# Gated attention and routed experts on one core: the order of work ahead of and in the slot loop

## Chip, cores and metric

The kernel runs on one NeuronCore of a Trainium2 chip. The metric is the time of one execution on the device, in microseconds (us); less is better.

## What is computed

The reference, cut to what matters here (B = 2, S = 512, D = 1024, 8 experts):

```python
def xattn(x1, x2):                      # per batch
    q1, q2 = fake_quant(x1, ...), fake_quant(x2, ...)
    return q1 @ q2
def ffn(x, W_gate, b_gate, W_e, b_e):
    logits = x @ W_gate + b_gate
    _, top_idx = top_k(logits, 2)
    y_all = relu(einsum('bsd,edh->bseh', x, W_e) + b_e)
    return take_along_axis(y_all, top_idx[..., None], axis=2).mean(axis=2)
x = x + tanh(g_xattn[0]) * xattn(layernorm(x), ctx)
x = x + tanh(g_ffn[0]) * ffn(layernorm(x), W_gate, b_gate, W_e, b_e)
```

## The kernel before, in words

The 1024 tokens are NT = 8 tiles of 128 rows, tiles 0 to 3 of the first batch (TPB = 4), 4 to 7 of the second. Per tile i the first part quantises x and the context, multiplies (attend, fold), adds to x (x_new, VectorE), takes the statistics (stats, scales), writes the normalised row y (normalise, ScalarE), stores y in DRAM (store_y, SP), transposes it on TensorE (transpose_y) and multiplies it with the gate's weights (gate).

Routing is done for two groups of four tiles, g = 0 and 1: select(g) finds the two best experts of every token on VectorE, counts(g) on TensorE counts by matmuls with a triangle of ones which place a token has among those of its expert, positions(g) reads that, and slot_matrix(g) (R) and make_onehot(i) make the operands with which place_rows on TensorE writes the list of tokens of each expert. A slot is 128 tokens of one expert: here 20 slots, numbered 0 to 19; slots 0 to 2 are expert 0's, and slots 3, 4, 6, 9, 13 and 16 are each the first of a next expert for which the one after it has still to be prepared (expert 7's slots come last).

Slots 0 and 1 don't wait for the whole list. oh_first (first_onehot, L906), the one-hot of the place in expert 0's column alone, gives by place_first the tokens of slot 0 from the first batch; first_rows writes their row numbers (sidx) and GpSimd gathers the rows of y (L517). ScalarE turns them from DRAM's order of quarters (put_in_order, L703), TensorE transposes them (turn_first), ScalarE writes yE_hi (evacuate_hi) and VectorE yE_lo (evacuate_lo): an fp32 product is made of three, hi by hi, hi by lo, lo by hi. place_second, second_rows and the gather at L522 do the same for slot 1, from both batches. products(q, ...) are the matmuls of slots 0 and 1.

Weights of an expert come in four pieces (chunks c) of 1 MB through stage. ScalarE writes w_hi from stage (split_hi), VectorE w_lo = stage - w_hi (split_lo, L944). Each of the two halves of w_hi and w_lo holds one expert. The half of w_hi for expert 1 lies in the same memory as xt, which holds x_new until its stores (store_x_new on SP, after add_rowsum on ScalarE for tiles 4 to 7) have landed (s_oi). The next piece of stage is loaded when both splits of the old one are done (load_w1 for expert 1).

From slot 2 on a loop runs on each engine, one step per slot, queue by queue: GpSimd gathers the rows of slot + 3 in four quarters (gather, L507) into one of two buffers, when ScalarE has written their numbers (gidx, pick_rows) and then adds the result to the output by an indirect DMA (scatter, L529). VectorE's step: yT_lo of slot + 1 (evacuate_lo, L938), the transposition of the rows of slot + 2 (turn_rows, L1067), in the first slot of an expert the four split_lo of the next expert, the bias (add_bias, L1072) when TensorE is done with the slot, relu and weight (weigh, L1076). ScalarE's step: when TensorE is done with slot - 1, yT_hi of slot + 1 (L687), gidx, and the four split_hi. TensorE: 48 matmuls of 512 columns a slot (L1419), which wait for yT_lo of the slot and piece by piece for w_lo. SP loads the four pieces of the expert after next as the splits free stage.

The order of every engine is written out by hand. Around the change it is, on VectorE:

```python
            x_new(7)
            stats(1, 7, 6)
            first_onehot(0)
            slot_matrix(0)
            scales(1, 7, 1, 6)
            first_rows()
```

and in VectorE's loop step:

```python
                turn_rows(q, turn + 1)
                with dve.If(nxt > 0):
                    for c in range(NCH):
                        split_lo(c, ...)
```

## Time and profile before

| | |
|---|---|
| time, median of 3 runs | 351.77 us (349.79 to 356.72) |
| the profiled execution | 349.38 us |
| its span | 347.6 us |
| mean granted clock of TensorE | 0.942 |
| busy: TensorE, VectorE, ScalarE, GpSimd | 90%, 70%, 42%, 50% |
| DMA | 81.48 MB, 234 GB/s |

The span runs from the first to the last instruction of the core; what is left of the execution's own time (1.8 us) lies around it. Busy shares are means over stages with different limits: the stage ahead of 131 us is many short instructions that wait for each other across engines, the loop behind it is mostly TensorE. An idle time in a timeline stands in brackets with the engine, tile and line that ended it; "issue" is time in which nothing that the profile shows was waited for. A piece of TensorE's timeline that starts before the last ends is no error, since matmuls are pipelined.

### The profile page before, as it was taken

Reading aid. Unit: us, or ns where it says so; the run is one execution under the profiler, and the core shown is the slowest. Engines: PE = TensorE matmul, PEld = TensorE weight load, DVE = VectorE, ACT = ScalarE, POOL = GpSimd, SP = SyncE. Lnnn points to the kernel's source line nnn. Section 1 sums busy time; section 2 is a strip of 40 time slices with the busy share of each in tenths; the row PEclk is TensorE's granted clock in tenths of the full one; section 3 lists DMA queues with packets and bytes.
Section 4 is the critical chain, followed back from the end, with each engine's and each line's share of the span. In section 5 each row is a group of like instructions: output and inputs, shape, how many; then the busy total and the mean of one; then the engine's idle time right before and its main releaser. Section 6 shows DMA issues by size and latency. Waiting matters only on the chain.

```text
span 347.6 us, 6194 instructions
## 1 busy us (share of the span) xinstructions
PE 311.7 (90%) x1591; PEld 238.8 (69%) x1598; DVE 244.2 (70%) x343; ACT 145.2 (42%) x144; POOL 174.3 (50%) x167
## 2 busy tenths in 40 slices
PE   4698999999899958999999979998999999999940
PEld 1243446769877837888888768877888888888830
DVE  2779999979669389598974965595639754964520
ACT  3768989854711461276446013701127114601100
POOL 5647534201010488684665566707748455847440
PEclk9989999988569996999999999999999999999995
DMA  6999937793726769889998995897559965546333
GB/s 222 414 410 385 389 122 240 300 312 117 201 104 184 285 227 326 248 246 414 315 387 206 334 326 121 184 367 241 121 121 256 396 142 154 125 71 154 63 86 60
DMA packets 19917, 81.48 MB, mean 234 GB/s; under 512 B 4160, under 2 KB 4160, under 8 KB 15808
## 3 DMA queue, kind: packets, MB, share of 16 engines
q1 hardware_dynamic: 12560, 58.76, 45.7%
q0 software_dynamic: 7200, 22.55, 28.4%
q8 instruction: 7, 0.11, 0.1%
q14 instruction: 6, 0.05, 0.0%
q10 hardware_dynamic: 144, 0.01, 0.0%
HBM read 62.43 MB, written 18.87 MB: 234 GB/s over the span
## 4 chain that ended last, share of the span: by engine, by line
PE 45%; DVE 23%; DMA 13%; issue 7%; ACT 4%; POOL 3%; DVEq 1%; SPq 1%; POOLq 0%; ACTq 0%
PE ps L1419 32%; DVE w_lo L944 8%; DMA out_dram<-res,sidx 4%; PE ps L1154 3%; DMA out_dram<-xt 3%; PE ps_q L1208 3%; PE ps_y L1183 2%; DVE st L771 2%; DMA stage<-in_ctx_dram 2%; DMA stage<-in_L_ffn_W_e_dram 2%; DVE res L1072 2%; PE ps_s L1208 2%; POOL y_rows L507 2%; DMA y_rows<-y_scratch,gidx 2%; DVE xt L827 1%
## 5 line engine op out<-in xcount | busy, mean ns | idle before, releaser
L507 POOL DMA_INDIRECT y_rows<-y_scratch,gidx x84 | 104.8, 1247 | 37.7 <-issue 25.3
L1419 PE MATMUL ps<-w_hi,yT_hi 128*128 x288 | 90.0, 394 | 8.7 <-DVE yT_lo L938 8.7
L1419 PE MATMUL ps<-w_lo,yT_hi 128*128 x288 | 89.6, 393 | 0.0
L1419 PE MATMUL ps<-w_hi,yT_lo 128*128 x288 | 89.4, 392 | 0.0
L687 ACT ACTIVATE yT_hi<-ps_y 128x1024 fp32r<-128x1024 f32 x20 | 20.5, 1027 | 132.8 <-PE ps L1419 76.8
L944 DVE TENSOR_TENSOR w_lo<-stage,w_hi 128x2048 f32 (+1 forms) x32 | 71.4, 2275 | 4.8 <-ACT w_hi L696 4.7
L1419 PEld LDWEIGHTS ps<-w_hi,yT_hi 128*128 128x128 f32 x288 | 54.4, 190 | 21.1 <-issue 10.1
L1419 PEld LDWEIGHTS ps<-w_hi,yT_lo 128*128 128x128 f32 x288 | 54.6, 190 | 11.5
L1419 PEld LDWEIGHTS ps<-w_lo,yT_hi 128*128 128x128 f32 x288 | 54.6, 190 | 11.5
L529 POOL DMA_INDIRECT out_dram<-res,sidx x20 | 32.3, 1616 | 59.3 <-DVE res L1076 47.5
L696 ACT ACTIVATE w_hi<-stage 128x2048 f32 (+1 forms) x28 | 51.6, 1906 | 5.9 <-DMA stage<-in_L_ffn_W_e_dram 3.5
L1072 DVE TENSOR_TENSOR res<-ps,bias 128x1024 f32<-128x1024 f32 x20 | 24.4, 1218 | 28.9 <-PE ps L1419 28.7
L1067 DVE STREAM_TRANSPOSE ps_y<-y_rows 128x1024 f32<-128x1024 f32 x20 | 25.2, 1260 | 21.7 <-DMA y_rows<-y_scratch,gidx 19.4
L1154 PE MATMUL ps<-q,q1T 128*128 128x512 bf16 x123 | 31.5, 394 | 1.0 <-DVE xt L827 0.5
L938 DVE TENSOR_TENSOR yT_lo<-ps_y,yT_hi 128x1024 fp32r<-128x1024 f32 x20 | 24.5, 1225 | 11.0 <-issue 8.2
L1154 PEld LDWEIGHTS ps<-q,q1T 128*128 128x128 bf16 x128 | 12.3, 101 | 16.0 <-issue 2.6
L771 DVE BATCH_NORM_STATS2 st<-xt 128x6 f32<-128x512 f32 x32 | 20.5, 682 | 0.4
L439 POOL TENSOR_SCALAR q<-u8c 128x1024 bf16<-128x1024 uint8 x14 | 14.9, 1069 | 9.2 <-ACT u8c L566 8.2
L566 ACT ACTIVATE u8c<-stage,par,drv 128x1024 uint8<-128x1024 f32 x14 | 16.7, 1229 | 0.8 <-DMA stage<-in_ctx_dram 0.8
L1076 DVE TENSOR_SCALAR res<-res,weight 128x1024 f32<-128x1024 f32 x18 | 13.7, 759 | 2.4
L1131 PE MATMUL ps<-fill,ident_b 128*128 128x512 bf16 x23 | 8.2, 522 | 4.8 <-POOL pick L433 4.8
L590 ACT ACTIVATE y<-xt,lnv 128x1024 f32<-128x1024 f32 x8 | 9.8, 1234 | 4.2 <-DVE lnv L796 4.2
(195 smaller groups left out, 295.3 us busy)
## 6 DMA issues: line engine op xcount, KB each, us to landing
stage<-in_L_ffn_W_e_dram SPq DMA_DIRECT2D x32, 1024.0 KB, 6.9
stage<-in_ctx_dram SPq DMA_DIRECT2D x16, 512.0 KB, 11.3
xt<-in_x_dram SPq DMA_DIRECT2D x8, 512.0 KB, 11.1
y_scratch<-y SPq DMA_DIRECT2D x8, 512.0 KB, 6.4
out_dram<-xt SPq DMA_DIRECT2D x8, 512.0 KB, 7.0
bias<-in_L_ffn_b_e_dram SPq DMA_DIRECT2D x8, 512.0 KB, 6.9
y_rows<-y_scratch,gidx POOLq DMA_INDIRECT x84
out_dram<-res,sidx POOLq DMA_INDIRECT x20
```

Of the source, the lines that this page charges most:

```text
L507: pool.indirect_dma_start(out=y_rows[q][:, b * QD:(b + 1) * QD], out_offset=None, in_=y_quarters[:, :], in_offset=bass.IndirectOffsetOnAxi ...
L529: pool.indirect_dma_start(out=out_rows[:, :], out_offset=bass.IndirectOffsetOnAxis(ap=sidx[:, q:q + 1], axis=0), in_=res[q][:, :], in_offs ...
L687: act.activation(into[:, :, :], ps_y[:, :, :], ACT.Copy).then_inc(s_eh, 1)
L696: act.activation(w_hi[:, bass.ds(half * WSZ + c * CW, CW)], stage[:, CK * c:CK * (c + 1), :].rearrange("p k h -> p (k h)"), ACT.Copy).then ...
L771: last = dve.bn_stats(st[:, which, h, :], xt[:, i, h * 512:(h + 1) * 512])
L938: dve.tensor_tensor(into[:, :, :], ps_y[:, :, :], hi[:, :, :].bitcast(f32), ALU.subtract).then_inc(s_el, 1)
L944: dve.tensor_tensor(w_lo[:, dst], stage[:, CK * c:CK * (c + 1), :].rearrange("p k h -> p (k h)"), w_hi[:, dst].bitcast(f32), ALU.subtract) ...
L1067: dve.transpose(ps_y[:, :, :].rearrange("p k (b r) -> p k b r", b=NQ), y_rows[q][:, :].rearrange("p (b k r) -> p k b r", b=NQ, k=KT)).then ...
L1072: dve.tensor_tensor(res[q][:, :], ps[q][:, :], bias[:, bass.ds(half * D, D)], ALU.add).then_inc(s_free, 1)
L1154: pe.matmul(ps[slab(i)][:, h * 512:(h + 1) * 512], q1T[:, i, k % KT, :], q2[:, k, h * 512:(h + 1) * 512], start=(k % KT == 0), stop=False)
L1208: last = pe.matmul(into, yT[YT_HOME[i]][:, k, :], wg[:, k, :], start=(k == 0), stop=(k == KT - 1))
L1419: last = pe.matmul(ps[q][:, h * 512:(h + 1) * 512], lhs[q][:, k, :], w[:, bass.ds(woff + k * D + h * 512, 512)], start=(k == 0 and lhs is ...
```

## The change

Edits of order and one of layout:

- VectorE, ahead of the loop: first_onehot(0) and slot_matrix(0) come ahead of x_new(7); first_rows is cut in two (row numbers early, weights later); split_lo(3) of expert 0 moves from behind evacuate_lo(0) to ahead of select(1).
- oh_first has the tile as its innermost index in place of the outermost, so place_first and place_second read their stationary operand with a step of 4 elements.
- TensorE: counts(0) ahead of the last four attends of tile 7; place_first directly behind fold(7); turn_first(0) ahead of gate(7), with its wait for keep_yT(7); place_rows of tile 3 and place_second one product later or earlier.
- ScalarE: the ordered rows of slot 0 and yE_hi ahead of the four add_rowsum; split_hi(0) of expert 1 ahead of evacuate_hi(1).
- SP: y of tiles 6 and 7 ahead of the third load of expert 1, and the stores of x_new ahead of its fourth.
- VectorE, in the loop: two of the four split_lo ahead of turn_rows and two behind it, each pair under its own test of nxt.

```diff
-        oh_first = [at(f"oh_first{b}", [P, TPB, P], bf16, WLO + 38 * KB + KB * b) for b in range(B)]
+        oh_first = [at(f"oh_first{b}", [P, P, TPB], bf16, WLO + 38 * KB + KB * b) for b in range(B)]
...
             for e in range(2):
                 load_bias(e)
-            store_y(5)
+            for i in range(TPB + 1, NT):
+                store_y(i)
             load_w1(2)
-            store_y(6)
-            store_y(7)
-            load_w1(3)
             for i in range(TPB, NT):
                 store_x_new(i)
+            load_w1(3)
...
-            for i in range(TPB, NT - 1):
-                add_rowsum(i)
             act.wait_ge(s_first, 16)
             put_in_order(0, res[0])
-            add_rowsum(NT - 1)
             evacuate_hi(0, yE_hi)
+            for i in range(TPB, NT):
+                add_rowsum(i)
             act.wait_ge(s_g[1], 16)
             put_in_order(1, y_rows[1])
+            act.wait_ge(s_oi, 16 * NT)
+            split_hi(0, 1, 32)
             evacuate_hi(1, yT_hi[1])
...
-            act.wait_ge(s_oi, 16 * NT)
-            for c in range(NCH):
+            for c in range(1, NCH):
                 split_hi(c, 1, 32)
...
-                dve.tensor_tensor(oh_first[b][:, :, :], pL[:, r, 0:1].to_broadcast([P, TPB, P]),
-                                  iota_pe[:, :, 0].unsqueeze(1).to_broadcast([P, TPB, P]), ALU.is_equal).then_inc(s_ohf, 1)
+                dve.tensor_tensor(oh_first[b][:, :, :], pL[:, r, 0].unsqueeze(1).to_broadcast([P, P, TPB]),
+                                  iota_pe[:, :, 0:TPB], ALU.is_equal).then_inc(s_ohf, 1)
...
                 rows_of(0, fl(V1F), A0)
+
+            def first_weights():
+
                 dve.tensor_scalar(fl(W0), fl(V1F), 0.0, dv(C2), ALU.is_lt, ALU.mult)
...
             dve.wait_ge(s_iota, 1)
-            x_new(7)
-            stats(1, 7, 6)
             first_onehot(0)
             slot_matrix(0)
+            x_new(7)
+            first_rows()
+            stats(1, 7, 6)
+            make_onehot(0)
             scales(1, 7, 1, 6)
-            first_rows()
-            for i in range(TPB):
+            first_weights()
+            for i in range(1, TPB):
                 make_onehot(i)
             split_lo(2, 3, slice(2 * CW, 3 * CW))
             read_rowsums(1)
+            split_lo(3, 4, slice(3 * CW, 4 * CW))
             select(1)
...
             evacuate_lo(0, yE_lo)
-            split_lo(3, 4, slice(3 * CW, 4 * CW))
...
                 dve.wait_ge(s_el, slot + 2)
+                def split_some(first, end):
+                    with dve.If(nxt > 0):
+                        for c in range(first, end):
+                            split_lo(c, nxt * NCH + c + 1, bass.ds((nxt & 1) * WSZ + c * CW, CW))
+
+                split_some(0, NCH // 2)
                 turn_rows(q, turn + 1)
-                with dve.If(nxt > 0):
-                    for c in range(NCH):
-                        split_lo(c, nxt * NCH + c + 1, bass.ds((nxt & 1) * WSZ + c * CW, CW))
+                split_some(NCH // 2, NCH)
...
             transpose_y(4)
+            counts(0)
             attend_quarters(7, 2, 4)
-            counts(0)
             fold(7)
+            place_first()
             transpose_y(5)
             gate(4)
             transpose_y(6)
             gate(5)
-            place_first()
             gate(6)
...
             place_rows(0, 0, 1)
+            pe.wait_ge(s_ye, NT)
+            turn_first(0)
             gate(7)
             place_rows(0, 1, 3)
-            pe.wait_ge(s_ye, NT)
             counts(1)
-            turn_first(0)
-            place_rows(0, 3, TPB)
...
-            products(0, yE_hi, w_hi, 0, 3)
+            products(0, yE_hi, w_hi, 0, 2)
+            place_rows(0, 3, TPB)
             place_second()
-            products(0, yE_hi, w_hi, 3, KT)
+            products(0, yE_hi, w_hi, 2, KT)
```

TensorE's queue from gate(7) on, before (yT_66 is the transposed y of tile 7, onehot_90 to 92 those of tiles 1 to 3, in_order_74 the ordered rows of slot 0):

```order
L1208 MATMUL ps_q<-wg,yT_66 128x8 x8
L1275 MATMUL ps<-R,onehot_90 128x8 x8
L1275 MATMUL ps<-R,onehot_91 128x8 x8
L1221 MATMUL ps_s<-sel,before 128x40
L1224 MATMUL ps_s<-sel,ones_b 128x40 x4
L1224 MATMUL ps_s<-sel,ones_b 128x32
L1224 MATMUL ps_s<-sel,ones_b 128x24
L1224 MATMUL ps_s<-sel,ones_b 128x16
L1224 MATMUL ps_s<-sel,ones_b 128x8
L1256 MATMUL ps_y<-ident_f,in_order_74 128x128 x8
L1275 MATMUL ps<-R,onehot_92 128x8 x8
L1263 MATMUL ps<-w_hi,yE_hi 128x512 x6
```

And after:

```order
L1264 MATMUL ps_y<-ident_f,in_order_74 128x128 x8
L1216 MATMUL ps_q<-wg,yT_66 128x8 x8
L1283 MATMUL ps<-R,onehot_90 128x8 x8
L1283 MATMUL ps<-R,onehot_91 128x8 x8
L1229 MATMUL ps_s<-sel,before 128x40
L1232 MATMUL ps_s<-sel,ones_b 128x40 x4
L1232 MATMUL ps_s<-sel,ones_b 128x32
L1232 MATMUL ps_s<-sel,ones_b 128x24
L1232 MATMUL ps_s<-sel,ones_b 128x16
L1232 MATMUL ps_s<-sel,ones_b 128x8
L1271 MATMUL ps<-w_hi,yE_hi 128x512 x4
L1283 MATMUL ps<-R,onehot_92 128x8 x8
```

The transposition of slot 0's rows is now ahead of gate(7) and of the counts that follow from it, and the last one-hot has gone behind the first four matmuls of slot 0.

VectorE's queue in a step of the loop, behind yT_lo, before (y_rows_56 are the gathered rows, ps_y their transposition; the ISA and REGISTER rows are its sequencer's):

```order
L938 TENSOR_TENSOR yT_lo_55<-ps_y,yT_hi_53 128x1024
L1065 ISA
L1067 STREAM_TRANSPOSE ps_y<-y_rows_56 128x1024
L1106 REGISTER_ALU x2
L1106 COMPARE_AND_BRANCH
L943 ISA
L944 REGISTER_ALU
L944 ISA
L944 TENSOR_TENSOR w_lo<-stage,w_hi 128x2048
L943 REGISTER_ALU
L944 ISA
L944 TENSOR_TENSOR w_lo<-stage,w_hi 128x2048
```

And after:

```order
L1110 REGISTER_ALU x2
L1110 COMPARE_AND_BRANCH
L945 ISA
L946 REGISTER_ALU
L946 ISA
L946 TENSOR_TENSOR w_lo<-stage,w_hi 128x2048
L945 REGISTER_ALU
L946 ISA
L946 TENSOR_TENSOR w_lo<-stage,w_hi 128x2048
L1110 UNCONDITIONAL_BRANCH
L1069 ISA
L1071 STREAM_TRANSPOSE ps_y<-y_rows_56 128x1024
```

The first pair of splits, with the branch and its registers, stands ahead of the transposition, and a second branch opens behind it.

ScalarE's queue behind the last keep_yT, before:

```order
L608 ACTIVATE xt<-xt,rsum 128x1024 x3
L703 ACTIVATE in_order_74<-res_58 128x512 x2
L608 ACTIVATE xt<-xt,rsum 128x1024
L687 ACTIVATE yE_hi<-ps_y 128x1024
L703 ACTIVATE res_58<-y_rows_57 128x512 x2
L687 ACTIVATE yT_hi_53<-ps_y 128x1024
L717 TENSOR_LOAD tab
```

And after:

```order
L702 ACTIVATE in_order_74<-res_58 128x512 x2
L686 ACTIVATE yE_hi<-ps_y 128x1024
L607 ACTIVATE xt<-xt,rsum 128x1024 x4
L702 ACTIVATE res_58<-y_rows_57 128x512 x2
L695 ACTIVATE w_hi<-stage 128x2048
L686 ACTIVATE yT_hi_53<-ps_y 128x1024
L717 TENSOR_LOAD tab
```

The ordered rows and yE_hi are ahead of all four rows of x_new, and one piece of w_hi stands ahead of yT_hi of slot 1 (yT_hi_53).

## Rows read from the trace of the kernel before

**Rows 1.** The page, section 2: granted clock of TensorE in 40 slices of 8.7 us.

```profile
PEclk9989999988569996999999999999999999999995
```

**Rows 2.** The chain that ended last, its longest piece (start us, us, what).

```profile
235.63 98.23 PE ps L1419 x432
```

**Rows 3.** Timeline of TensorE, the loop: start us, us, instruction, [idle before <-releaser].

```profile
131.24 1.22 PE L1419 MATMUL ps<-w_hi,yT_hi 128*128 x2 [5.22 <-DVE yT_lo L938]
...
201.76 0.73 PE L1419 MATMUL ps<-w_hi,yT_hi 128*128 x2 [2.52 <-DVE yT_lo L938]
...
235.63 0.72 PE L1419 MATMUL ps<-w_hi,yT_hi 128*128 x2 [0.92 <-DVE yT_lo L938]
```

**Rows 4.** Timeline of VectorE ahead of slot 2.

```profile
120.81 2.29 DVE L944 TENSOR_TENSOR w_lo<-stage,w_hi 128x2048 fp32r<-128x2048 f32 x1 [4.73 <-ACT w_hi L696]
...
127.14 1.25 DVE L1067 STREAM_TRANSPOSE ps_y<-y_rows 128x1024 f32<-128x1024 f32 x1
```

**Rows 5.** Timeline of ScalarE ahead of slot 2.

```profile
116.38 0.32 ACT L691 ACTIVATE gidx<-qidx 128x4 uint32 x2 [1.66 <-issue]
118.86 7.33 ACT L696 ACTIVATE w_hi<-stage 128x2048 fp32r<-128x2048 f32 x4 [2.16 <-DMA out_dram<-xt]
```

**Rows 6.** Timeline of SP's queue.

```profile
108.02 2.35 SPq L340 DMA_DIRECT2D out_dram<-xt  x4
```

**Rows 7.** Windows: stretch, length, busy of PE, PEld, DVE, ACT, POOL (x), PEclk, DMA, GB/s.

```profile
131.20:136.40 5.20, 5.16 (x12) 4.13 (x13) 4.78 (x3) 1.12 (x2) 4.29 (x4) 0.51 1.05 294
137.00:142.20 5.20, 5.20 (x25) 4.26 (x24) 2.87 (x3) 0.00 (x0) 3.94 (x4) 1.00 1.08 362
...
201.80:207.00 5.20, 5.20 (x23) 4.31 (x24) 3.73 (x5) 1.23 (x2) 3.98 (x5) 1.00 1.04 321
```

**Rows 8.** Timeline of VectorE, the step of slot 6.

```profile
187.66 1.26 DVE L1067 STREAM_TRANSPOSE ps_y<-y_rows 128x1024 f32<-128x1024 f32 x1 [4.94 <-DMA y_rows<-y_scratch,gidx]
```

**Rows 9.** Timeline of ScalarE, weights of slots 4 and 6.

```profile
161.85 1.92 ACT L696 ACTIVATE w_hi<-stage 128x2048 f32 x1 [1.21 <-DMA stage<-in_L_ffn_W_e_dram]
...
179.63 7.32 ACT L696 ACTIVATE w_hi<-stage 128x2048 f32 x4
```

**Rows 10.** Timeline of VectorE, steps of slots 2 to 5.

```profile
143.03 1.26 DVE L1067 STREAM_TRANSPOSE ps_y<-y_rows 128x1024 f32<-128x1024 f32 x1 [1.86 <-DMA y_rows<-y_scratch,gidx]
...
147.31 1.23 DVE L938 TENSOR_TENSOR yT_lo<-ps_y,yT_hi 128x1024 fp32r<-128x1024 f32 x1 [0.23 <-issue]
...
164.25 8.86 DVE L944 TENSOR_TENSOR w_lo<-stage,w_hi 128x2048 f32 x4
...
175.42 1.22 DVE L938 TENSOR_TENSOR yT_lo<-ps_y,yT_hi 128x1024 fp32r<-128x1024 f32 x1 [0.23 <-issue]
```

**Rows 11.** Timeline of TensorE, start of slot 6.

```profile
177.27 0.63 PE L1419 MATMUL ps<-w_hi,yT_hi 128*128 x2
```

**Rows 12.** Timeline of GpSimd's queue, first gather of slot 4.

```profile
131.54 2.24 POOL L507 DMA_INDIRECT y_rows<-y_scratch,gidx  x1 [0.30 <-issue]
```

**Rows 13.** Timeline of TensorE ahead of slot 0's products.

```profile
88.72 3.57 PE L1208 MATMUL ps_q<-wg,yT 128*128 128x8 f32 x16
...
94.86 0.19 PE L1221 MATMUL ps_s<-sel,before 128*128 128x40 bf16 x1 [1.61 <-issue]
...
95.13 1.95 PE L1256 MATMUL ps_y<-ident_f,in_order 128*128 128x128 f32 x8
96.87 0.64 PE L1275 MATMUL ps<-R,onehot 128*128 128x8 f16 x8
98.28 2.90 PE L1263 MATMUL ps<-w_hi,yE_hi 128*128 128x512 f32 x6 [0.78 <-ACT yE_hi L687]
```

**Rows 14.** Groups by line and form, 76 to 112 us: oh_first.

```profile
L906 DVE TENSOR_TENSOR oh_first<-pL,iota_pe 128x512 bf16<-128x512 bf16 x2 | 2.2, 1084 | 0.1
```

**Rows 15.** DMA issues, us to landing: slot 0's gather.

```profile
res<-y_scratch,sidx POOLq DMA_INDIRECT x1, 5.1
```

**Rows 16.** Timeline of VectorE: slot 0's row numbers.

```profile
84.64 0.15 DVE L915 TENSOR_SCALAR sidx<-early 128x1 uint32<-128x1 f32 x1
```

More of the change, by code:

```diff
@@ L1237, in place_first @@
                     for c in (0, TPB):
-                        last = pe.matmul(first_in, oh_first[0][:, i, :], R[:, i * E, c:c + 1],
+                        last = pe.matmul(first_in, oh_first[0][:, :, i], R[:, i * E, c:c + 1],
                                          start=(i == 0 and c == 0), stop=(i == TPB - 1 and c == TPB))
@@ L1246, in place_second @@
                 for i in range(NT):
-                    last = pe.matmul(second_in, oh_first[i // TPB][:, i % TPB, :], R[:, i * E, 0:2],
+                    last = pe.matmul(second_in, oh_first[i // TPB][:, :, i % TPB], R[:, i * E, 0:2],
                                      start=(i == 0), stop=(i == NT - 1))
```

## The prediction

> **What bounds the kernel now.** I read the page first, then the timeline of TensorE for its gaps, then the timelines of the engines that ended them, and last the windows for the granted clock. The page shows the clock at full speed but for the stretch ahead of slot 0's products and a dent near 130 us [rows 1]. From slot 11 on TensorE never waits: one piece of 432 matmuls from 235.63 to 333.98 us [rows 2]. A slot is 48 matmuls, so 98.23 / 9 = 10.9 us. Nothing in the last nine slots can be won by order; what can be won lies ahead of them, in three gaps inside the slot loop [rows 3] and on the way to the first of them.
>
> Gap A, 5.22 us ahead of slot 2. It ends with yT_lo of slot 2 on VectorE, which follows the transposition of y_rows at 127.14, which stands behind the first two w_lo pieces of expert 1; the first of these waited 4.73 us for w_hi [rows 4]. ScalarE could write that w_hi only at 118.86, when the stores of x_new had landed (2.16 us of wait are put to out_dram) [rows 5]: expert 1's w_hi lies where x_new lay. The stores went out at 108.02 [rows 6], because SP stood at the fourth load of expert 1 ahead of them, which waits for VectorE's last split of expert 0. Gap A also costs clock: in the 5.2 us behind it 12 matmuls run at 0.51 of full speed, against 25 in as long a stretch later. That is 2.4 us lost [rows 7].
>
> Gap B, 2.52 us ahead of slot 8, ends with yT_lo of slot 8. In VectorE's step for slot 6, the first of an expert, the transposition waited 4.94 us for gathered rows until 187.66 [rows 8], and the four w_lo pieces stood behind it. Gap C, 0.92 us ahead of slot 11, has the same form. After gap B the clock stayed full [rows 7].
>
> **The change part by part.**
>
> *Two w_lo pieces ahead of the transposition in the loop.* Four pieces take 8.86 us [rows 10], so two take 4.4. From 182.7 VectorE runs them in place of waiting: ScalarE writes w_hi from 179.63 at 1.83 us a piece [rows 9], two by 183.3, so they hardly wait. They end at 187.2, the rows are there at 187.66, the other two end near 193.3 instead of 197.7. yT_lo of slot 8 is written by about 197, before the end of slot 7 at 199.1. Gap B goes: -2.52. Gap C too: the gather behind it is issued after the scatter of an earlier slot, which now goes out some 4 us sooner: -0.92. The slow first pairs after both gaps (0.73 and 0.72 against 0.63 [rows 3, 11]) give 0.2. What is late next is TensorE itself. In steps whose rows are there at once the transposition comes 4.4 us later; its reader, ScalarE's yT_hi, waits for the end of TensorE's slot anyway, and of the 10.9 us about 1.2 us of cover stay. Bounds: -3.6 to 0.
>
> *The price in the loop.* Each step tests its branch twice. Before, the branch is issued while the transposition runs; now the first stands open behind the wait for yT_lo. No row shows it; the nearest is the 0.23 us of issue ahead of yT_lo [rows 10]. I take 0.3 us a step, between 0 and three times that row.
>
> *Where that price decides.* Slots 3 and 4 are each the first of an expert. VectorE works through both steps without a pause: from yT_lo at 147.31 to the end of yT_lo for slot 6 (175.42 + 1.22) are 29.3 us [rows 10], and with the 0.53 us of hand-over that lies between yT_lo's end and the first matmul after gap A it allows slot 6 at 177.17; TensorE began it at 177.27 by its own work [rows 11]. Slack 0.1 us. This stretch is VectorE's own work, which the change reorders but doesn't shorten. So any head start that TensorE wins before slot 6 is lost there, unless the stretch itself begins sooner. It begins when the rows of slot 4 are there: the transposition at 143.03 waited 1.86 us for them [rows 10]. They come from GpSimd's queue, which from 116.85 on issues twelve gathers and a scatter nearly end to end, the last four from 131.54 [rows 12]. The queue starts when ScalarE writes gidx at 116.38 [rows 5], behind the second turn_first.
>
> *Ahead of the loop: does gidx come sooner?* counts(0) ahead of the last attends gives VectorE its input 1.6 us sooner. first_onehot and the slot matrix, now ahead of x_new 7, end near 78.7 and put it off by 0.2. The new layout of oh_first is read and written in steps that no row shows; between the old 1.08 us [rows 14] and half of it, I take 0.9, near the one row there is. TensorE has place_first behind fold(7), waits there some 0.4 us and begins transpose_y(5) about 0.8 us late; so comes all behind it, turn_first(0) at 89.7. Slot 0's gather follows sidx, now at 80.6 instead of 84.64 [rows 16]; at 5.1 us from issue to landing [rows 15] the rows lie there by 87, and ScalarE orders them straight behind the last keep_yT, from 89.4 to 90.5. turn_first(0), 1.95 us at half clock, ends at 91.8; gate(7), 3.57 us, which stood ahead of it and ended at 92.28, now ends at 95.2. From gate(7) to counts(1) are 2.6 us of select on VectorE (92.28 to 94.86), so counts(1) comes at 97.8 and slot 0's products at 98.2, against 98.28 [rows 13]. What the early yE_hi wins, the late select gives back: 0. place_rows of tile 3, 0.64 us [rows 13], now stands behind the start of the products; with the 0.1 won it shifts slots 0 and 1, turn_first(1) and gidx by 0.4 to 0.5 (gidx 116.8). Bounds: -1.3 to +1.3, by whether 1.95 + 0.64 us of this run at half or at full clock.
>
> The Trainium skill, SBUF — State Buffer, "Door 1: The DMA port swizzle", says that accesses which each cross into a new 16-byte line pay a penalty. By it the new oh_first, which still reads pL in such steps, would stay at 1.08 us and place_first be 0.2 later. No row here shows the new layout.
>
> *Stores and loads in their new order, split_lo(3) early.* split_lo(3), 2.3 us, falls into VectorE's wait for gate(7): free. The stores of x_new go out from 94 to 97.5 and land by 105. ScalarE writes the first w_hi of expert 1 near 109.5, behind the ordered rows of slot 1 (it is ahead of yT_hi(1) in its queue, which needs turn_first(1) at 113.1, so it holds nobody). VectorE's first split then runs at 116.9 instead of 120.81 and the second at 121.2. The transposition of slot 2 now waits for its gather: four issues of 1.25 us from 117.2, two of them a us longer since they lie beside splits (as the 2.24 us in [rows 12]), landing near 125.8. With the 4.1 us from transposition to matmul [rows 3, 4], slot 2 begins at 129.9: a wait of 3.4 us instead of 5.22. If the clock holds, slot 3 begins 3.4 us sooner than before and slot 6 could at 174. But GpSimd's queue starts 0.4 us later and has as many splits beside it, four, so the rows of slot 4 are there at 143 as before, and slot 6 begins at 177.17 + 0.6 (two branches): +0.5 against 177.27. The head start is worth nothing.
>
> *Clock.* TensorE waits 3.4 us ahead of slot 2 and 3 us or so ahead of slot 6. It fell after a wait of 5.22 us and not after 2.52 [rows 3, 7]. A fall ahead of slot 2 costs nothing (slot 6 covers it); one at slot 6 costs the 2.4 us above. I give it one in four: +0.6.
>
> The Trainium skill, TensorE: Matmul & The Clock Gate, "HAM oscillation — how this bites in real kernels", says that waits between bursts of matmuls throttle the array again, so that each burst starts cold. By it slot 6 would start cold and the sum be 1.8 us more. The trace has one wait that did this and one that didn't.
>
> **Sum**, against the profiled execution (349.38 us, of it 347.6 span): -2.52 - 0.92 - 0.2 + 0.5 + 0.6 = -2.5, so 346.8. The median of the runs shown is 351.77, the lowest 349.79, 0.4 over the profiled one; I add 1.0 for that spread: 347.8.
>
> **The rivals.**
> 1. *The head start survives*, because GpSimd's queue or the splits go faster than I sum. For it: in what started the stretch, the rows of slot 4 were only some 0.3 us ahead of TensorE. Against it: twelve gathers end to end. 347.8 - 3.4 - 0.6 = 343.8.
> 2. *The gaps return as one.* Those of slots 8 and 11 go, but the wait ahead of slot 6 has the branches at their upper bound (1.4 for 0.5) and the clock falls there in full (2.4 for 0.6): 347.8 + 0.9 + 1.8 = 350.5.
> 3. *Slower: the transposition behind two splits holds TensorE.* It must end before TensorE's slot does and now ends 9.7 us into 10.9. In slot 4 ScalarE waited for the weights themselves, 1.21 us for the second piece [rows 9]. Where w_hi of the first two pieces comes over 1.2 us later than VectorE asks for it, each further us is one of TensorE. With 3 us beyond that in four of the six steps: 347.8 + 12 = 360. Against it: at 179.63 all four w_hi go end to end (7.32 us) [rows 9].
> 4. *It doesn't do what it says:* sidx of slot 0 is early, but turn_first(0) waits on PE for the ordered rows, holds gate(7), and select(1), gidx and slot 6 come 3 us later: 347.8 + 3 = 350.8.
>
> **How the numbers follow.** Forecast 0.52, rival 1 0.19, rival 2 0.14, rival 3 0.05, rival 4 0.10. Range 343.0 to 352.0: it takes in rivals 1, 2 and 4 with the spread of the runs. Some 2% (7 us) is what a measurement of this kernel can tell from no change. Faster by more asks for 344.7 or less, rival 1 and little else: 0.20. Slower by more: rival 3 and a tail of 4, 0.06. Within it: 0.74.
>
> **What would show it.** Right: no wait of TensorE ahead of slots 8 and 11 and a transposition without wait in slot 6; stores of x_new out before 100; slot 0's products within 1 us of 98.3; slot 2 near 130; a new wait of 2 to 4 us ahead of slot 6, which starts between 177 and 178.5. Wrong: slot 6 before 176 without a wait (rival 1), ScalarE's yT_hi waiting for the transposition in expert steps with TensorE idle (rival 3), gidx after 118 (rival 4).

## The result and the profile after

| | before | after |
|---|---|---|
| median (range) of 9 runs each, us | 351.17 (349.79 to 356.72) | 353.82 (350.61 to 355.25) |
| ratio, 95% interval | | 1.0082 (1.0048 to 1.0115) |
| profiled execution, its span, us | 349.38, 347.6 | 353.82, 352.0 |
| mean granted clock | 0.942 | 0.932 |

The change makes the kernel slower by 0.8%, where 347.8 us was forecast. The interval lies above 1, but the loss is less than the 2% that the prediction names as what a measurement can tell. Medians are over all runs of a kernel, while ratios and intervals, on both sides, leave out the runs that are more than 1.5% above the fastest of their kernel. Each ratio is against the kernel before on the same chip, whose own median lies between 351.2 and 353.4 us.

The two profiles overstate the difference. That of after is its median run, that of before lies 1.8 us below its median; of the 4.4 us between them, 2.65 lie between the medians.

The page's clock row answers to [rows 1]: the dip is wider, and the one near 140 us is still there.

```profile
PEclk9999999986557997899999999999999999999995
```

TensorE's timeline of the loop answers to [rows 3] (start us, us, instruction, [idle before <-releaser]); no other row of the loop has a wait.

```profile
138.22 1.21 PE L1427 MATMUL ps<-w_hi,yT_hi 128*128 x2 [6.56 <-DVE yT_lo L940]
...
185.26 0.72 PE L1427 MATMUL ps<-w_hi,yT_hi 128*128 x2 [0.80 <-DVE yT_lo L940]
```

The waits ahead of slots 8 and 11 are gone, and from slot 6 to the end of the span now lie 352.0 - 185.26 = 166.7 us against 347.6 - 177.27 = 170.3 [rows 11]: -3.6. But slot 2 starts at 138.22 instead of 131.24 and slot 6 at 185.26 instead of 177.27. The loss lies ahead of slot 2. TensorE's timeline there answers to [rows 13]:

```profile
78.80 0.40 PE L1246 MATMUL ps<-R,oh_first 128*128 128x1 f16 x8 [0.65 <-issue]
...
81.68 1.62 PE L1191 MATMUL ps_y<-ident_f,y 128*128 128x128 f32 x8
83.09 6.83 PE L1216 MATMUL ps_q<-wg,yT 128*128 128x8 f32 x32
...
93.47 1.94 PE L1264 MATMUL ps_y<-ident_f,in_order 128*128 128x128 f32 x8 [0.38 <-ACT in_order L702]
95.21 3.42 PE L1216 MATMUL ps_q<-wg,yT 128*128 128x8 f32 x16
98.47 1.09 PE L1283 MATMUL ps<-R,onehot 128*128 128x8 f16 x16
101.16 0.21 PE L1229 MATMUL ps_s<-sel,before 128*128 128x40 bf16 x1 [1.59 <-DVE sel L855]
...
101.45 2.05 PE L1271 MATMUL ps<-w_hi,yE_hi 128*128 128x512 f32 x4
103.31 0.67 PE L1283 MATMUL ps<-R,onehot 128*128 128x8 f16 x8
104.33 0.40 PE L1255 MATMUL ps_s<-R,oh_first 128*128 128x2 f16 x8 [0.36 <-DVE R L891]
104.59 5.20 PE L1271 MATMUL ps<-w_hi,yE_hi 128*128 128x512 f32 x12
```

The waits ahead of the first product are near those foreseen (0.65 ahead of place_first, 0.38 for the ordered rows, 1.59 for select); the 0.36 us that place_second (L1255) waits for R was not foreseen. Nor were the durations: gates 5 and 6 (83.09) take 6.83 us together, where one gate at half clock was 3.57 us before [rows 13], and the twelve products at 104.59 still run at half clock. Windows of 1 us give the two edges (columns as in [rows 7]); of after

```profile
82.00:83.00 1.00, 1.00 (x7) 1.00 (x6) 0.93 (x4) 0.24 (x1) 0.61 (x1) 0.52 0.08 33
109.00:110.00 1.00, 1.00 (x5) 0.84 (x4) 0.86 (x6) 0.00 (x0) 0.00 (x0) 0.83 0.65 213
```

and of before

```profile
85.00:86.00 1.00, 1.00 (x8) 1.00 (x8) 0.97 (x3) 0.41 (x1) 0.31 (x1) 0.54 0.02 8
102.00:103.00 1.00, 1.00 (x6) 0.83 (x5) 0.96 (x5) 0.00 (x0) 0.00 (x0) 0.92 0.00 0
```

A mean of 0.54 in a window that ends at 0.50 means a fall 0.08 us into it; a mean of 0.92 that began at 0.50 a return 0.16 us into it. So the clock was at its lower level (1.2 of 2.4 GHz) from 85.1 to 102.2 before, and from 82.0 to 109.3 after: 27.3 us for 17.1. In both kernels TensorE was busy all through the window in which it fell.

The lower clock isn't one profile's accident. The mean granted clock of every run is on record: 0.922 to 0.941 in the nine runs of after (mean 0.930), and 0.923 to 0.952 in the 65 runs of the kernel before that were made beside the experiments (mean 0.936, and 0.935 to 0.937 on each of their chips). Span times mean clock, an estimate of the span at full clock throughout, is 326.8 us in the mean for after and 328.1 for before. By this estimate the changed kernel has 1.3 us less to do, and the lower clock costs it some 2.4 us.

In the two profiles slot 1 ends 5.6 us late (131.65 for 126.03). The other 1.4 us up to slot 2 are its longer wait, 6.56 us for 5.22. GpSimd's queue, the first gathers of the loop:

```profile
121.24 0.95 POOL L506 DMA_INDIRECT y_rows<-y_scratch,gidx  x1 [13.43 <-ACT gidx L690]
122.50 2.23 POOL L506 DMA_INDIRECT y_rows<-y_scratch,gidx  x1 [0.30 <-issue]
125.03 0.95 POOL L506 DMA_INDIRECT y_rows<-y_scratch,gidx  x1 [0.30 <-issue]
126.28 2.57 POOL L506 DMA_INDIRECT y_rows<-y_scratch,gidx  x1 [0.30 <-issue]
```

SP's queue (after [rows 6]), and VectorE's transposition (after [rows 4]):

```profile
97.53 3.45 SPq L340 DMA_DIRECT2D out_dram<-xt  x4
...
124.08 19.68 SPq L382 DMA_DIRECT2D stage<-in_L_ffn_W_e_dram  x4
```

```profile
134.10 1.26 DVE L1071 STREAM_TRANSPOSE ps_y<-y_rows 128x1024 f32<-128x1024 f32 x1 [6.07 <-DMA y_rows<-y_scratch,gidx]
```

The stores leave 10.5 us sooner, as intended, and the transposition no longer stands behind splits. But the last of the four gathers is issued at 126.3 to 128.85, behind the first load of expert 2 (124.08), and its rows are there only at 134.1, 5.2 us after the issue ended.

Between slots 2 and 6 another 1.0 us goes. VectorE's timeline of slots 4 to 8:

```profile
154.71 1.23 DVE L940 TENSOR_TENSOR yT_lo<-ps_y,yT_hi 128x1024 fp32r<-128x1024 f32 x1 [0.24 <-issue]
156.53 4.50 DVE L946 TENSOR_TENSOR w_lo<-stage,w_hi 128x2048 f32 x2 [0.60 <-DVE yT_lo L940]
...
183.49 1.23 DVE L940 TENSOR_TENSOR yT_lo<-ps_y,yT_hi 128x1024 fp32r<-128x1024 f32 x1 [0.23 <-issue]
...
197.70 1.25 DVE L1071 STREAM_TRANSPOSE ps_y<-y_rows 128x1024 f32<-128x1024 f32 x1
```

In the same step of the kernel before, yT_lo was followed by the transposition:

```profile
148.79 1.26 DVE L1067 STREAM_TRANSPOSE ps_y<-y_rows 128x1024 f32<-128x1024 f32 x1 [0.26 <-DVE yT_lo L938]
```

The chain from yT_lo of slot 4 to the end of that of slot 6 takes 183.49 + 1.23 - 154.71 = 30.0 us, against 29.3: the branch shows as 0.60 us behind yT_lo instead of 0.26, once for slot 4 and once for slot 5. The transposition at 197.70 (slot 6's step) has no wait, where before it had 4.94 [rows 8].

The account of the two profiles: +5.6 (slot 1 ends) +1.4 (longer wait) +1.0 (to slot 6) -3.6 (slots 8 and 11) = +4.4 us of span, 352.0 - 347.6.

### The profile page after: what moved, and what is told of

Read it like the earlier page. It is cut to its first block, busy times and chain, and to the rows that moved or that the text cites. A ratio compares the mean times of both kernels' runs of the same rounds, so it can differ in the third digit from the quotient of the medians.

```text
span 352.0 us, 6225 instructions
## 1 busy us (share of the span) xinstructions
PE 316.5 (90%) x1597; PEld 242.6 (69%) x1598; DVE 243.9 (69%) x343; ACT 144.8 (41%) x144; POOL 189.8 (54%) x167
## 3 DMA queue, kind: packets, MB, share of 16 engines
q0 software_dynamic: 7200, 22.55, 27.9%
## 4 chain that ended last, share of the span: by engine, by line
PE 64%; DVE 15%; DMA 6%; ACT 4%; issue 4%; POOL 2%; DVEq 1%; ACTq 1%; SPq 0%; POOLq 0%
PE ps L1427 47%; PE ps L1271 3%; PE ps_q L1216 3%; PE ps L1162 3%; PE ps_y L1191 3%; DMA stage<-in_L_ffn_W_e_dram 2%; DMA y_rows<-y_scratch,gidx 2%; DVE st L770 2%; DMA stage<-in_ctx_dram 2%; PE ps_s L1216 2%; DVE w_lo L946 2%; DVE xt L826 1%; ACT u8c L565 1%; POOL y_rows L506 1%; ACT w_hi L695 1%
## 5 line engine op out<-in xcount | busy, mean ns | idle before, releaser
L506 POOL DMA_INDIRECT y_rows<-y_scratch,gidx x84 | 118.4, 1410 | 39.4 <-issue 25.0
L1427 PE MATMUL ps<-w_lo,yT_hi 128*128 x288 | 89.6, 392 | 0.0
L528 POOL DMA_INDIRECT out_dram<-res,sidx x20 | 34.3, 1714 | 43.0 <-DVE res L1080 30.9
L1080 DVE TENSOR_SCALAR res<-res,weight 128x1024 f32<-128x1024 f32 x18 | 13.9, 771 | 2.4
L521 POOL DMA_INDIRECT y_rows<-y_scratch,sidx x1 | 1.4, 1400 | 23.8 <-DVE sidx L914 23.8
L596 ACT ACTIVATE yT<-ps_y 128x1024 f32<-128x1024 f32 x8 | 8.2, 1020 | 12.7 <-PE ps_y L1191 12.6
```

The lines of the kernel that those rows point to most:

```text
L506: pool.indirect_dma_start(out=y_rows[q][:, b * QD:(b + 1) * QD], out_offset=None, in_=y_quarters[:, :], in_offset=bass.IndirectOffsetOnAxi ...
L528: pool.indirect_dma_start(out=out_rows[:, :], out_offset=bass.IndirectOffsetOnAxis(ap=sidx[:, q:q + 1], axis=0), in_=res[q][:, :], in_offs ...
L1427: last = pe.matmul(ps[q][:, h * 512:(h + 1) * 512], lhs[q][:, k, :], w[:, bass.ds(woff + k * D + h * 512, 512)], start=(k == 0 and lhs is ...
```

## The experiments

**The loop edit alone, and all without it.** The first is the kernel before with this, the second the changed kernel without it:

```diff
-                turn_rows(q, turn + 1)
-                with dve.If(nxt > 0):
-                    for c in range(NCH): split_lo(c, ...)
+                split_some(0, NCH // 2)
+                turn_rows(q, turn + 1)
+                split_some(NCH // 2, NCH)
```

> Only the loop edit: two w_lo pieces ahead of the transposition, two behind, all else as before. Theory A (the loss lies ahead of the loop, the loop edit pays as its terms say): the waits ahead of slots 8 and 11 (2.52 and 0.92 us) go, slot 6 begins 0.5 to 0.8 us later with a wait of that size, so 2.5 to 3 us less than before, ratio 0.992. Theory B (the loop edit itself costs: the second branch and w_hi waits in six steps): at least 2 us more than before, ratio 1.006 or above.

> Everything of the change but the loop edit. Theory A: slot 2 begins 6 to 7 us later than before and the waits ahead of slots 8 and 11 are back, 0 to 3.5 us of them; time 5 to 8 us over before, ratio 1.015 to 1.022. Theory B: all of the change's loss is the loop's, ratio 1.00.

Measured: 348.09 us, ratio 0.987 (0.978 to 0.997), and 357.21 us, ratio 1.010 (1.000 to 1.020). Alone, slot 6 starts 1.0 us later (178.24) and no wait of TensorE over 0.4 us is left behind it; without it the wait ahead of slot 8 is back (2.58 us). The edit pays, as theory A says. The rest of the change loses, but less than theory A's 1.015 to 1.022, and the interval touches 1; slot 2 did start 7.8 us late in its profile (139.05).

**The order of TensorE and VectorE ahead of slot 0 (the front, from here on) as before.** SP's and ScalarE's order, the early split_lo(3) and the loop edit stay. The edit, cut (make_onehot(0), counts(0) and place_first go back too):

```diff
-            first_onehot(0); slot_matrix(0); x_new(7); first_rows(); ...
+            x_new(7); stats(1, 7, 6); first_onehot(0); slot_matrix(0); ...
-            turn_first(0)
             gate(7)
             place_rows(0, 1, 3)
             counts(1)
+            turn_first(0)
+            place_rows(0, 3, TPB)
-            products(0, yE_hi, w_hi, 0, 2)
-            place_rows(0, 3, TPB)
+            products(0, yE_hi, w_hi, 0, 3)
```

> The change with the order of TensorE and VectorE ahead of slot 0's products put back (x_new 7, stats, first_onehot, place_first, gate(7), counts(1), turn_first(0), place_rows as before); the early split_lo(3), SP's and ScalarE's order and the loop edit stay. Theory A1 (the clock's earlier fall comes from the new front): half clock begins near 85 again, slot 0's products near 98.3, slot 1 ends near 126; the time falls to 345 to 348. Theory A2 (the clock's fall wanders from run to run by itself, whatever the order): products as late as 101 in some, time as after within 2 us. Theory C (slot 2's rows land late because the gather lies beside expert 2's load): a wait of 4 to 6 us ahead of slot 2 in spite of w_hi being ready, and slot 2 not before 130.

Measured: 349.5 us (345.5 to 352.7), ratio 0.989 (0.983 to 0.995), against 1.008: these two orders carry the loss. With the loop edit alone the ratio was 0.987, so the early stores, ScalarE's order and the early split_lo(3) show no gain. The time lies between the forecasts of A1 and A2, and the one profile looks like A2: its clock fell at 82.6 and its products began at 100.41. Theory C came true: slot 2 still waited 6.29 us.

**Expert 2's load behind slot 2's gather**, in the changed kernel and in the last one.

```diff
             sp.wait_ge(s_tab, 1)
+            sp.wait_ge(s_g[0], 16 * NQ)
             with sp.Fori(2, E) as n:
```

> The change, and SP's first load of expert 2 waits until slot 2's rows have landed. Theory C: the transposition for slot 2 begins 3 to 5 us after the gather's first issue plus 4 issues, near 130.5 instead of 134.1, TensorE's wait ahead of slot 2 is 2.5 to 3.5 us instead of 6.56 and slot 2 begins at about 134.5; slot 6 gains less, 1 to 3 us. Rival (the rows are late because GpSimd's own issue is slow beside the splits): transposition at 133 or later in spite of the free queues, and time as after or above.

> e3_front_undone, and SP's first load of expert 2 waits until slot 2's rows have landed. Theory C (the gather for slot 2 loses to the 1 MB load): wait ahead of slot 2 about 3 us instead of 6.29, clock not or hardly lowered there, time 1.5 to 3 us under e3 for the same fall of the clock ahead of slot 0. Theory of the prediction (a head start is lost in VectorE's steps for slots 3 and 4): of the 3 us at slot 2 at most 2 are left at the start of slot 6, which has a wait ahead of it.

Measured: 353.03 us, ratio 1.007 (1.000 to 1.014), and 349.95, ratio 0.995 (0.986 to 1.004). VectorE's and TensorE's timelines of the first:

```profile
130.66 1.26 DVE L1072 STREAM_TRANSPOSE ps_y<-y_rows 128x1024 f32<-128x1024 f32 x1 [2.62 <-DMA y_rows<-y_scratch,gidx]
```

```profile
134.81 0.72 PE L1428 MATMUL ps<-w_hi,yT_hi 128*128 x2 [3.17 <-DVE yT_lo L941]
...
148.26 0.72 PE L1428 MATMUL ps<-w_hi,yT_hi 128*128 x2 [2.26 <-DVE yT_lo L941]
...
183.10 0.73 PE L1428 MATMUL ps<-w_hi,yT_hi 128*128 x2 [1.88 <-DVE yT_lo L941]
```

With gather issues at the same times (the last ends at 128.86) the transposition finds its rows 1.8 us after the issue instead of 5.2, and the wait ahead of slot 2 is 3.17, near the 3.4 forecast. With the old order ahead of slot 0 it falls from 6.29 to 3.30. So it is the load that the gather loses to. But slots 3 and 6 now wait. Of the 3.4 us won at slot 2 in the first profile, 2.2 are left at slot 6 (183.10 for 185.26) and 1.1 at the end of the span; the clock fell once more behind slot 6 (184.3 to 187.7). In the second, counted from the end of slot 1, it is 3.0, 1.8 and 1.4. So in the profiles the head start is about halved, not lost, and the forecast that it is worth nothing isn't borne out as it stands. The median of the second (349.95) is no lower than without the wait (349.5), where 1.5 to 3 us were expected.

**Slot 0's products in one piece**: in the changed kernel with the load behind the gather; in the changed kernel by itself; and, the other way round, the broken order (4 matmuls, place_rows, place_second, the rest) put into the kernel before with the loop edit.

```diff
             place_rows(0, 1, 3)
+            place_rows(0, 3, TPB)
             counts(1)
-            products(0, yE_hi, w_hi, 0, 2)
-            place_rows(0, 3, TPB)
+            products(0, yE_hi, w_hi, 0, 3)
             place_second()
-            products(0, yE_hi, w_hi, 2, KT)
+            products(0, yE_hi, w_hi, 3, KT)
```

> e4_load_behind_gather, and place_rows of tile 3 stands ahead of counts(1) (in the wait for select) and place_second behind three steps of products, so that slot 0's products begin with 6 matmuls and one short break. Theory D (the clock comes back late because slot 0's products are broken up after 4 matmuls): half clock ends 4 to 6 us behind the first product instead of 7.6, slot 1 ends 1.5 to 2.5 us sooner than in e4 (131.6), time 1 to 2 us under e4. Rival (the clock's return follows only where its own steps happen to fall): first product to return anything from 4 to 8 us, time within 1 us of e4.

> The changed kernel, of it only slot 0's products as before: place_rows of tile 3 ahead of counts(1), three products (6 matmuls) in front of place_second. The load of expert 2 is where the change has it. Theory (the four matmuls in front of the small place_rows and place_second keep the clock low for longer): the clock is back at full by 103 to 105 instead of 109.2, slot 1 ends near 127 instead of 131.65, the time is 347.5 to 350.5, ratio to the kernel before 0.985 to 0.995. Rival (where the clock falls wanders from run to run, 82 to 86 us, and the order of the products has no part in it): back within 8 us of the first product whether it fell early or late, time 352 to 355, ratio 1.0 to 1.01.

> The kernel before with the loop edit, and slot 0's products in the changed order: two products (4 matmuls), place_rows of tile 3, place_second, then the rest. Nothing else of the front is touched. Theory (the broken products hold the clock down): the clock is back 7 us or more behind the first product (106 or later, before 102.1 with the first product at 98.3), slot 1 ends 2 to 4 us later than in the kernel with the loop edit alone, time 350 to 352, ratio 0.993 to 1.0. Rival (the wandering of the fall alone): back near 102, time 348, ratio 0.983 to 0.99.

Measured: 347.58 us, ratio 0.988 (0.980 to 0.997), where the same kernel with broken products had 1.007 (1.000 to 1.014); 350.93, ratio 1.000 (0.997 to 1.003), where the changed kernel had 1.008 (1.005 to 1.012); and 350.39, ratio 0.992 (0.988 to 0.995), where the loop edit alone had 0.987 (0.978 to 0.997). With the new order ahead of slot 0 whole products are faster, clear of the noise; with the old one the intervals overlap, and nothing is shown.

The profiles say only in part why. TensorE's timeline with the load behind the gather and broken products:

```profile
81.66 1.75 PE L1192 MATMUL ps_y<-ident_f,y 128*128 128x128 f32 x8
83.19 6.84 PE L1217 MATMUL ps_q<-wg,yT 128*128 128x8 f32 x32
...
93.58 1.94 PE L1265 MATMUL ps_y<-ident_f,in_order 128*128 128x128 f32 x8 [0.39 <-ACT in_order L703]
```

and with whole ones:

```profile
81.66 1.07 PE L1192 MATMUL ps_y<-ident_f,y 128*128 128x128 f32 x8
82.57 3.95 PE L1217 MATMUL ps_q<-wg,yT 128*128 128x8 f32 x32
...
90.06 1.94 PE L1265 MATMUL ps_y<-ident_f,in_order 128*128 128x128 f32 x8 [0.40 <-ACT in_order L703]
...
98.05 2.91 PE L1272 MATMUL ps<-w_hi,yE_hi 128*128 128x512 f32 x6
```

Up to the transposition of the ordered rows both have the same instructions, and at 81.66 they are at the same place to 0.01 us. Yet the clock fell at 81.9 in one and at 85.7 in the other, and that alone makes 3.5 us (93.58 to 90.06). The order of the products comes behind the fall and can't have moved it in that execution. All profiles of kernels without idle matmuls, by windows of 1 us ("broken" or "whole" are slot 0's products; the front is the new one unless the name says undone, before or loop edit alone):

| kernel | fell | first product | back, after first product | slot 1 ends, after first product |
|---|---|---|---|---|
| before | 85.1 | 98.28 | 3.9 | 27.8 |
| loop edit alone | 85.3 | 98.18 | 4.2 | 27.9 |
| front undone | 82.6 | 100.41 | 6.1 | 28.8 |
| front undone, load behind gather | 84.8 | 98.63 | 3.3 | 27.8 |
| load behind gather, products whole | 85.7 | 98.05 | 4.8 | 28.3 |
| products whole, by itself | 87.3 | 99.50 | 4.9 | 28.3 |
| after (broken, as the next two) | 82.0 | 101.45 | 7.9 | 30.2 |
| all but the loop edit | 83.3 | 102.84 | 7.7 | 30.1 |
| load behind gather | 81.9 | 101.56 | 7.6 | 30.1 |
| loop edit alone, products broken | 83.2 | 97.05 | 6.6 | 29.3 |

(The front undone was profiled in a somewhat longer execution, 350.89 us.) With whole products the clock is back after 3.3 to 6.1 us, with broken ones after 6.6 to 7.9. From first product to the end of slot 1 that is 29.3 to 30.2 us for 27.8 to 28.8; 0.67 of it is place_rows, which only changed sides, so the broken order goes with some 1.1 us.

That it is the cause is not quite shown, since the two groups also differ in when the clock fell. All four profiles with broken products are among those with an early fall (81.9 to 83.3); the one with whole products and as early a fall (82.6) needed 6.1 us, not far from the 6.6. One pair is free of this: from the fall to the first product are 13.8 us in "front undone, load behind gather" and 13.9 in "loop edit alone, products broken", and the clock was back 3.3 us behind the first product with whole products and 6.6 with broken ones. It is one pair.

The third kernel was expected to have its clock back at 106 or later, which its early first product did not allow (103.7), and slot 1 to end 2 to 4 us later than with the loop edit alone; it ended 0.2 us later (126.3), in a profile in which all of this part stood 1.5 us earlier. The median meets the 350 to 352. Its profile shows a stall of 3.3 us that no other has (VectorE in slot 3, put to a remote event), so its span decides nothing. The second kernel had its clock back at 104.4, as its theory says, but 350.93 lies between the theory's range and the rival's. The first gained 5.5 us where 1 to 2 were expected, and 3.5 of them are, in the profiles, the later fall.

Does the fall have a place of its own in either order? By the clock of the profile it fell at 82.0, 83.3, 81.9, 85.7, 87.3 with the new front, and at 85.1, 85.3, 82.6, 84.8, 83.2 with the old. Three profiles stand 1.3 to 1.5 us later or earlier than their likes at place_first already (80.12, 80.29 and 81.79). With that taken off the falls are 81.9 to 82.0 in the three with the new front and broken products, 85.7 and 85.8 in the two with whole ones, and 82.6 to 85.3 in the five with the old front. That may be chance or something that goes with the kernel; with one profile a kernel it stays open. Between the runs of one kernel the clock differs as well: the nine means of after, 0.922 to 0.941, stand for 41 to 55 us at half clock (an estimate, twice the missing share times the span).

**Idle matmuls against the fall of the clock.** They write a bank that the next real matmul clears and add nothing to the result. Four kernels have them: the changed kernel with the load behind the gather; the kernel before with the loop edit; the changed kernel with the old front; and the changed kernel with whole products and the load behind the gather. The edit in the first, without the 3 ahead of place_first:

```diff
             gate(5)
+            keep_clock(4, ps[1][:, 0:512])
             gate(6)
+            keep_clock(4, ps[1][:, 0:512])
...
             place_rows(0, 0, 1)
+            keep_clock(4, ps[0][:, 0:512])
...
             gate(7)
+            keep_clock(4, ps[0][:, 0:512])
             place_rows(0, 1, 3)
+            keep_clock(4, ps[0][:, 0:512])
```

> e4_load_behind_gather with idle matmuls of 512 columns (ones times identity into a bank that is free there) put between the gates: 3 ahead of place_first, 4 each behind gate(5), gate(6), the first place_rows, gate(7) and the next place_rows; 23 in all, 5 us at full clock. Theory A (what is lost ahead of slot 0 is clock, because TensorE has only short matmuls there): no fall of the clock between 78 and 110 or a much shorter one; slot 0's products begin by 97 instead of 101.4, slot 1 ends by 123 to 126 instead of 131.6, time 5 or more us under e4. Rival (the stretch is bound by the waits between engines, and the clock only looks like the cause): products begin at 101 or later.

> The kernel before with the loop edit alone (e1_loop_alone), and the same idle matmuls: 4 each behind gate(5), gate(6), the first place_rows, gate(7) and the next place_rows, 3 ahead of slot 0's products. Theory A: the clock holds here too, slot 0's products begin by 95 instead of 98.2, slot 1 ends by 120 to 122, time 3 to 6 us under e1 and less spread between runs. Rival: they cost their 5 us and give nothing, time at or over e1.

> The changed kernel with the order of TensorE and VectorE ahead of slot 0 as before (early stores of x_new, early split_lo(3), ScalarE's order and the loop edit kept), and idle matmuls that hold the clock: 4 of 512 columns each behind gate(5), gate(6), the first place_rows, gate(7) and the next place_rows, 3 ahead of the products. Theory (the only thing wrong with the changed kernel is the clock ahead of slot 0, and the head start on slot 2 is capped by VectorE's chain of slots 3 and 4): 344.5 to 346.5, no better than the old front with the loop edit and the same idle matmuls (345.05). Rival (the early stores are worth something once the clock is held): 342 to 344.

> The changed kernel with SP's wait for the gather, slot 0's products unbroken, and idle matmuls of 512 columns that hold the clock (3 ahead of place_first, 4 each behind gate(5), gate(6), the first place_rows, gate(7), and ahead of counts(1)). Theory (the loss of the change is the clock ahead of slot 0; with it held, VectorE's chain through slots 3 and 4 is what is left, and it sets slot 6 at 176 to 178.5 whatever the head start): 344.5 to 347.5, ratio 0.978 to 0.987, as good as the old front with the loop edit and idle matmuls (345.05) and not better. Rival (with the clock held, the early yE_hi and early splits are worth their 3 us): 341 to 343.5, slot 6 before 175.

Measured, in this order: 348.22 us, ratio 0.987 (0.978 to 0.997), where the same kernel without them had 1.007 (1.000 to 1.014); 345.05, ratio 0.979 (0.970 to 0.988), the fastest of all, where the loop edit alone had 0.987 (0.978 to 0.997); 354.9, with five of six runs at 354.3 to 356.4 and one at 348.44, which is inconclusive; and 349.73, ratio 0.985 (0.979 to 0.990), with seven runs from 345.8 to 352.6 and one at 464.6 (mean clock 0.642), which no profile explains. TensorE's timeline of the second:

```profile
88.45 2.34 PE L1212 MATMUL ps_q<-wg,yT 128*128 128x8 f32 x16
...
98.11 1.62 PE L1267 MATMUL ps<-w_hi,yE_hi 128*128 128x512 f32 x6
...
99.79 2.52 PE L1267 MATMUL ps<-w_hi,yE_hi 128*128 128x512 f32 x10
```

and two of its windows:

```profile
89.00:90.00 1.00, 1.00 (x9) 1.00 (x9) 0.00 (x0) 1.00 (x1) 0.00 (x0) 0.82 0.70 106
96.00:97.00 1.00, 1.00 (x11) 1.00 (x10) 0.96 (x2) 0.06 (x1) 0.00 (x0) 0.77 0.65 266
```

The clock still fell, but for a shorter time: from 89.6 to 96.5 here, where it was down from 85.3 to 102.4 with the loop edit alone, and from 97.0 to 100.4 in the first kernel, where it was down from 81.9 to 109.2. The six first products take 1.62 us instead of 2.90 [rows 13]. They begin no sooner (98.11 for 98.18; by 95 was expected), since the idle matmuls take the time that the clock gives back, and slot 1 ends 1.7 us sooner (124.39; 120 to 122 was expected). In the first kernel products begin at 98.74 instead of 101.56 and slot 1 ends 4.9 us sooner (126.73). So the half clock ahead of slot 0 is real time in the new order, clear of the noise; in the old one the intervals overlap, though three of the four runs (344.8 to 345.1) lie under all four with the loop edit alone (347.2 to 350.1); the fourth took 352.4.

The new order ahead of slot 0 is not shown to be faster than the old one when both have idle matmuls: 0.985 against 0.979, with overlapping intervals. Nor is this a comparison at full clock. The one profile of the fourth kernel, of a run of 351.34 us, has the clock down from 87.5 to 97.7 and from 101.1 to 104.5, its products begin at 103.64, and slot 6 starts at 183.00, outside the 176 to 178.5 of its theory. In the second kernel slot 6 starts at 176.34, 1.9 us sooner than with the loop edit alone. What holds in all of these is the length of VectorE's chain (30.0 us from yT_lo of slot 4 to the end of that of slot 6 in after, with the loop edit alone, with the load behind the gather, and in this second kernel); where it begins moves.

## Why the prediction was wrong

**The step that failed** is "Ahead of the loop", its sum "What the early yE_hi wins, the late select gives back: 0 ... Bounds: -1.3 to +1.3, by whether 1.95 + 0.64 us of this run at half or at full clock". It took the place where the clock falls (85 us) from one profile and let only two instructions move across it. After's fall at 82.0 put gates 5 and 6, the transposition and all up to the products at half clock: first product at 101.45, not 98.2, and gidx at 120.77, not 116.8. Over the runs the clock's share is smaller but there: mean 0.930 against 0.936, some 2.4 us by the estimate above. As an order of instructions the step was about right: where the clock fell at 85.7 the products of the new order began at 98.05.

**Second, in the same step**, place_rows of tile 3 behind the first products was costed at its own 0.64 us. With it the clock came back 7.9 us behind the first product instead of 3.9, and place_second waited 0.36 us for R: 30.2 us to the end of slot 1 instead of 27.8. Whole products brought the ratio from 1.008 to 1.000, and from 1.007 to 0.988 with the load behind the gather. How much of the late return is due to the broken order, and how much to the early fall, is not settled. A profile of before, in which the products are whole, has no row for that.

**Third, "landing near 125.8" and slot 2 at 129.9 with a wait of 3.4 us.** With the load out of the way the wait is 3.2 to 3.3 and slot 2 starts at 129.6 to 129.9 where the products start near 98. In the changed kernel expert 2's load leaves ahead of the last gather, and the wait is 6.56. I counted each queue's issues and took the landing from a stretch where no load ran beside it. The same paragraph has the rows of slot 4 "at 143 as before"; they were there at 149.27 in after, 4.4 us of it by the late gidx and 1.9 by a later landing behind gidx.

**The base.** The sum starts from a profiled execution of 349.38 us and adds 1.0 us for the spread of the runs. The median of nine is 351.17, so 1.8 was due; this term is 0.8 us of the 6.0 us by which the forecast missed.

**Right:** the waits of slots 8 and 11 (-3.6 forecast and measured); 0.3 us a branch (0.34); the stores (97.53); select's lateness (1.59 us ahead of counts(1)). oh_first takes 1.03 and 1.06 us in its new layout and took 1.08: my 0.9 was off by 0.15. By the Trainium skill, SBUF — State Buffer, "Door 1: The DMA port swizzle", it would stay at 1.08, since the read of pL still crosses into a new line each time; the trace agrees to 0.05 us. Reading oh_first in steps of 4 elements has a small price that the prediction leaves out: TensorE's load of one such operand takes 0.12 us instead of 0.10.

**Not tested by the change:** that a head start on slot 2 is worth nothing. The changed kernel had none. With the load behind the gather 2.2 of 3.4 us were left at slot 6, and 1.8 of 3.0 with the old front.

**Clock at slot 6:** no fall in after (0.80 us of wait). The Trainium skill, TensorE: Matmul & The Clock Gate, "HAM oscillation — how this bites in real kernels", describes a kernel in which every burst of matmuls after a wait starts cold. The runs here show both, bursts at half clock and at full clock after waits of about the same length: see the last section.

**The rivals.** None came as written. The fourth has the right end (gidx at 120.77, after its mark of 118) by another way: turn_first(0) waited only 0.38 us for the ordered rows, and the half clock did most of the rest. The second's 2.4 us at slot 6 didn't come, the third's stall neither: ScalarE's yT_hi never held TensorE in an expert's step.

**What stays open.** The new front with whole products measured 1.000 (0.997 to 1.003) and the old front 0.989 (0.983 to 0.995); the table puts the new front's products 0.3 us late at an equal place of the fall, the wait at slot 2 is alike in both (6.41 and 6.29), and no run says where the rest comes from. The intervals with the load behind the gather (0.988 with whole products, 0.995 with the old front) don't show this difference. Why the clock is lower in the runs of after is shown in part only: the broken products go with it, and whether the new front also brings the fall forward can't be told from ten profiles. A second profile of one kernel would tell what is chance. A kernel with the new front in which only turn_first(0) goes back behind counts(1) was not tried.

## What to carry to other kernels

Look at the granted clock around the stretch that you reorder, in more than one profile, before you price an instruction in it: where it falls or returns can be worth more than the instructions moved. Start a sum from the median run, or say how far the profiled one is from it. Be wary of small matmuls or a wait among the first large ones behind a slow stretch; here they went with a late return of the clock. Where the stretch can't be filled, try idle matmuls: they were worth 2% in one kernel here and 0.8%, within the noise, in another. Before a transfer is made early, find which other queue it will meet, and whether the next chain of one engine's own work takes part of the gain.

## What the runs showed of the hardware

- Two kernels with the same instructions up to there, at the same place to 0.01 us, lost their clock at 81.9 us in one and 85.7 in the other, with TensorE busy throughout; over ten profiles the fall lay between 81.9 and 87.3. The mean clock of nine runs of one kernel went from 0.922 to 0.941.
- A wait's length doesn't tell whether the clock falls behind it. After 3.17 us ahead of slot 2 it stayed full (23 matmuls in 5.2 us, load behind the gather), after 2.27 us ahead of slot 6 it fell (16 matmuls, granted 0.67, the same kernel with idle matmuls):

```profile
134.80:140.00 5.20, 5.19 (x23) 4.31 (x24) 1.82 (x2) 0.00 (x0) 4.16 (x4) 1.00 1.01 344
```

```profile
178.80:184.00 5.20, 5.18 (x16) 4.13 (x17) 2.63 (x4) 1.45 (x3) 3.98 (x5) 0.67 1.01 377
```

- The issue of an indirect gather takes 0.95 us on GpSimd, and in most cases 1.9 to 3.0 beside VectorE's w_lo splits. Its rows were there 1.8 us after the last issue with no load beside it, and 5.2 us after it beside a load of 1 MB pieces.
